# Two layers of spatial attention over 32 images: lane 1 normalised when its rows are split, and attended on two tiles at a time

## The chip, the cores and the metric

The kernel runs on one core of one Trainium2 chip. The metric is the device time of one execution in microseconds (us). Before the change three runs gave 1569.89, 1571.02 and 1573.38 us, with a median of 1571.02 us. The core has TensorE for matrix products (PE in the rows of a profile; its weight loads are PEld), VectorE (DVE), ScalarE (ACT), GpSimd (POOL) and SyncE (SP). Each engine takes its own instructions in order, and they meet at semaphores. Here SP does nothing but issue DMAs.

## The reference

The input is x of shape (32, 128, 32, 32): 32 images, 128 channels (C), 1024 positions (N). Two layers follow one another on each image:

```
h    = group_norm(x, 32 groups) * gn_w + gn_b
q,k,v = split(qkv_w @ h + qkv_b)                    # 128 channels each
attn = softmax(q^T k * 128**-0.5, over keys)        # 1024 x 1024
x1   = x + proj_w @ (v attn^T) + proj_b

q,k  = Wq @ x1 + bq, Wk @ x1 + bk                   # 16 channels each
v    = Wv @ x1 + bv                                 # 128 channels
attn = softmax(q^T k, over keys)                    # 1024 x 1024
out  = x1 + gamma * (v attn^T)
```

Operands of the large products are split into a half-precision head and a half-precision tail (value minus head), and a product takes three matmuls: head by head, head by tail, tail by head.

## The kernel before

**Tiles.** A tile is 128 queries of one image in one layer: 8 tiles for an image in a layer, 512 in all. For a tile the kernel makes 128 x 1024 scores in PSUM, their row maximum, the exponent, a head and a tail of the exponents in half precision (`rows`, 128 x 2048), a DMA transpose of those rows into `pt` with the keys in partitions, and the product of `pt` with the values into `mixed`.

**Lanes and slots.** The program is laid out by hand in slots. In a slot each of two lanes starts one tile. Lane 0 holds layer 0 and lane 1 holds layer 1 of an earlier image, except in the first eight slots (layer 0 of images 0 and 1 on both lanes) and the last eight (layer 1 of images 30 and 31 on both lanes). A tile of slot s has its scores made by PE at the end of slot s-1, its rows in slot s, its transpose issued by SP in slot s (lane 1) or s+1 (lane 0), and its product in slot s+3 (`ATTEND`). There it is also normalised and turned back, and in slot s+4 (`ADD`) it is added to the residual. One image of each layer takes eight slots.

**Lane 1 in a slot.** The scores stay in the PSUM tile `scores1` until the rows are done. `row_max` (DVE, line 572) takes the maximum, `exponent1` (ACT, line 457) writes the exponents over the scores, `head_row1` (ACT, line 465) writes the head with the constant factor 4096, `tail_row1` (DVE, line 589) writes the tail. Only then may PE write the next tile's scores: `score1` waits on `row_tailed[1]` through `scores_free` (line 785).

**Lane 0 in a slot.** `row_max` and `exp_bias` (DVE, lines 572 and 578), `exponent0` (ACT, line 452) into `prob`, and the head and the tail on POOL (lines 353 and 358).

**The product.** `attend` (PE, lines 823 to 825) has 8 blocks of keys by 3 matmuls. The transposed rows are the stationary operand and the values with a column of ones are the moving one, 129 or 128 columns wide. The queries come out in partitions, and the ones' column gives the row sum. `invert` (DVE, line 584) takes its reciprocal, `norm` (ACT, line 481) scales 128 x 128 values, `back` (PE, line 843) turns them so that channels are in partitions, and `x1_out` or `y_out` (DVE, lines 599 and 609) adds the residual.

**Order on the engines.** DVE in a slot: maximum of lane 1; tail of a projection of the slot before (`W`: lines 642, 649, 657); maximum and bias of lane 0; the adds of both lanes; `tail_row1`; the reciprocals; half of the statistics of a later image (`STATS`, line 616, in two of eight slots); small group-norm steps (`GN`, in two more). ACT: `exponent1`, `head_row1`, `exponent0`, then copies and `norm`s, then evictions of projections. PE: both products of slot-3, a projection of the values or of layer 1, a projection of q or k, group-norm products, the scores of the next slot, the turns back. Image 2 is an exception: its group-norm products stand behind the scores of slots 0 and 1 (`GN_BEHIND`).

**Buffers.** `pt` has 4 places in each lane (`RING`), `rows` has 3 in each.

## Time and profile before

| | |
|---|---|
| three runs, median | 1571.02 us |
| the profiled execution | 1575.76 us, its span 1573.7 us |
| mean granted TensorE clock | 0.989 |
| busy in the span | PE 94%, PEld 71%, DVE 82%, ACT 77%, POOL 79% |
| DMA queue of SP (transposes) | 1066688 packets, 270.42 MB |
| chain that ended last | SP's queue 66%, PE 17%, issue 5%, DVE 4% |

The profile is of one execution. Its page gives the busy share of each engine, the chain of work that ended last, followed back from the end, and the costliest groups of instructions by source line. The trace behind it can be asked for single instructions in order of time, for who waited for whom, and for the busy time of a stretch. Matmuls overlap in their records, so a matmul's duration is not the time it takes from the next one; the distance between two starts is.

### The profile page before, as it was taken

Reading aid. Unit: us, or ns where it says so; the run is one execution under the profiler, and the core shown is the slowest. Engines: PE = TensorE matmul, PEld = TensorE weight load, DVE = VectorE, ACT = ScalarE, POOL = GpSimd, SP = SyncE. Lnnn points to the kernel's source line nnn. Section 1 sums busy time; section 2 is a strip of 40 time slices with the busy share of each in tenths; the row PEclk is TensorE's granted clock in tenths of the full one; section 3 lists DMA queues with packets and bytes.
Section 4 is the critical chain, followed back from the end, with each engine's and each line's share of the span. In section 5 each row is a group of like instructions: output and inputs, shape, how many; then the busy total and the mean of one; then the engine's idle time right before and its main releaser. Section 6 shows DMA issues by size and latency. Waiting matters only on the chain.

```text
span 1573.7 us, 43918 instructions
## 1 busy us (share of the span) xinstructions
PE 1482.2 (94%) x16777; PEld 1116.9 (71%) x16777; DVE 1285.6 (82%) x2508; ACT 1218.2 (77%) x1698; POOL 1240.4 (79%) x1027
## 2 busy tenths in 40 slices
PE   4899999999999999999899999999999999999977
PEld 2577777776777777777677777677777777777766
DVE  5678888888888888888788888888888878888885
ACT  3578878887877887878788887887878878888774
POOL 3788888888878887878788888788788878888653
PEclk9899999999999999999999999999999999999999
DMA  3799999999999999999999999999999999999999
GB/s 76 135 161 199 203 197 204 198 206 204 198 195 194 207 203 203 202 193 209 189 202 211 202 194 202 196 202 203 195 199 210 203 190 204 203 193 199 192 200 181
DMA packets 1081437, 305.21 MB, mean 194 GB/s; under 512 B 1068272, under 2 KB 1068944, under 8 KB 1081232
## 3 DMA queue, kind: packets, MB, share of 16 engines
q1 hardware_dynamic: 1066688, 270.42, 105.4%
q10 hardware_dynamic: 14544, 31.99, 6.0%
q8 instruction: 137, 2.24, 0.5%
q14 instruction: 68, 0.56, 0.1%
HBM read 17.13 MB, written 16.78 MB: 22 GB/s over the span
## 4 chain that ended last, share of the span: by engine, by line
SPq 66%; PE 17%; issue 5%; DVE 4%; DMA 3%; ACT 2%; POOL 1%; DVEq 0%; POOLq 0%; ACTq 0%
SPq L299 66%; DMA pt<-rows 3%; PE mixed L823 3%; PE mixed L825 3%; PE mixed L824 3%; PE scores L778 2%; DVE nmax L572 2%; PE scores L779 1%; PE scores L780 1%; DVE rows L589 1%; PE scores L808 1%; PE bank_w L889 1%; PE bank_w L897 1%; ACT scores L457 1%; POOL rows L358 1%
## 5 line engine op out<-in xcount | busy, mean ns | idle before, releaser
L823 PE MATMUL mixed<-v_head,pt 128*128 128x129 f16 x4096 | 719.5, 222 | 35.7 <-DMA pt<-rows 34.6
L572 DVE TENSOR_REDUCE nmax<-scores 128x1 f32<-128x1024 f32 x512 | 620.5, 1217 | 154.8 <-PE scores L808 141.8
L825 PE MATMUL mixed<-v_head,pt 128*128 128x129 f16 x4096 | 718.7, 220 | 0.0
L824 PE MATMUL mixed<-v_tail,pt 128*128 128x128 f16 x4096 | 718.7, 219 | 0.0
L358 POOL TENSOR_TENSOR rows<-prob,rows 128x1024 f16<-128x1024 f32 x256 | 545.4, 2130 | 21.3
L353 POOL TENSOR_SCALAR rows<-prob 128x1024 f16<-128x1024 f32 x256 | 267.9, 1046 | 233.4 <-ACT prob L452 229.9
L457 ACT ACTIVATE scores<-scores,nmax 128x1024 f32<-128x1024 f32 x256 | 278.7, 1089 | 204.2 <-DVE nmax L572 204.2
L823 PEld LDWEIGHTS mixed<-v_head,pt 128*128 128x128 f16 x4096 | 399.0, 97 | 47.1 <-DMA pt<-rows 45.6
L824 PEld LDWEIGHTS mixed<-v_tail,pt 128*128 128x128 f16 x4096 | 405.7, 99 | 2.3
L825 PEld LDWEIGHTS mixed<-v_head,pt 128*128 128x128 f16 x4096 | 397.0, 97 | 0.0
L589 DVE SCALAR_TENSOR_TENSOR rows<-scores,rows 128x1024 f16<-128x1024 f32 x256 | 313.0, 1222 | 35.6 <-ACT rows L465 35.4
L452 ACT ACTIVATE prob<-scores,ebias 128x1024 f32<-128x1024 f32 x256 | 283.9, 1109 | 2.1 <-DVE ebias L578 2.1
L465 ACT ACTIVATE rows<-scores 128x1024 f16<-128x1024 f32 x256 | 262.2, 1024 | 24.8 <-ACT scores L457 1.5
L481 ACT ACTIVATE normal<-mixed,rinv 128x128 f32<-128x128 f32 x512 | 162.5, 364 | 101.6 <-DVE rinv L584 99.8
L778 PE MATMUL scores<-qk_head 128*128 128x512 f16 x512 | 198.6, 388 | 8.2 <-DVE rows L589 6.9
L779 PE MATMUL scores<-qk_tail,qk_head 128*128 128x512 f16 x512 | 196.2, 383 | 0.0
L780 PE MATMUL scores<-qk_head,qk_tail 128*128 128x512 f16 x512 | 196.0, 383 | 0.0
L420 POOL TENSOR_TENSOR qk_tail<-qk,qk_head 128x512 f16<-128x512 f32 x124 | 143.7, 1159 | 10.3
L778 PEld LDWEIGHTS scores<-qk_head 128*128 128x128 f16 x512 | 50.0, 98 | 97.9 <-issue 55.9
L808 PE MATMUL scores<-qk 64*128 64x512 f16 x512 | 98.9, 386 | 20.3 <-DVE rows L589 17.8
L843 PEld LDWEIGHTS bank_t<-ident,normal 128*128 128x128 f32 x512 | 71.6, 141 | 55.5 <-ACT normal L481 5.2
L843 PE MATMUL bank_t<-ident,normal 128*128 128x128 f32 x512 | 99.4, 275 | 3.8 <-ACT normal L481 3.7
(110 smaller groups left out, 1852.8 us busy)
## 6 DMA issues: line engine op xcount, KB each, us to landing
out_dram<-y ACTq DMA_DIRECT2D x64, 256.0 KB, 3.8
x_raw<-in_x_dram ACTq DMA_DIRECT2D x29, 512.0 KB, 5.2
pt<-rows SPq DMA_TRANSPOSE x512, 5.4
x_raw<-in_x_dram SPq DMA_DIRECT2D x3, 512.0 KB, 4.4
w_qkv<-in_L_conv_qkv_w_dram SPq DMA_DIRECT2D x3, 64.0 KB, 4.1
b_qk<-in_L_conv_bk_dram SPq DMA_DIRECT2D x8, 0.1 KB, 2.3
b_qk<-in_L_conv_bq_dram SPq DMA_DIRECT2D x8, 0.1 KB, 1.9
w_proj<-in_L_conv_proj_w_dram SPq DMA_DIRECT2D x1, 64.0 KB, 4.8
```

The costliest lines, as they stand in the source:

```text
L299: sp.dma_start_transpose(pt[l][:, i % RING, :, :], rows[l][:, i % ROWS, :, :].rearrange("p s n -> p (s n)")).then_inc(swung[l][i % RING], 16)
L353: nc.gpsimd.tensor_scalar(rows[0][:, tile.i % ROWS, 0, :], prob[:, tile.i % 2, :], 1.0, 1.0, ALU.mult, ALU.mult).then_inc(row_headed[0], 1)
L358: nc.gpsimd.tensor_tensor(rows[0][:, tile.i % ROWS, 1, :], prob[:, tile.i % 2, :], rows[0][:, tile.i % ROWS, 0, :], ALU.subtract).then_inc ...
L452: nc.scalar.activation(prob[:, tile.i % 2, :], scores[0][:, :], ACT.Exp, bias=ebias[:, tile.i % TILES:tile.i % TILES + 1], scale=1.0).then ...
L457: nc.scalar.activation(scores[1][:, :], scores[1][:, :], ACT.Exp, bias=nmax[1][:, tile.i % TILES:tile.i % TILES + 1], scale=1.0).then_inc( ...
L465: nc.scalar.activation(rows[1][:, tile.i % ROWS, 0, :], scores[1][:, :], ACT.Copy, scale=P_UP).then_inc(row_headed[1], 1)
L572: nc.vector.reduce_max(nmax[l][:, tile.i % TILES:tile.i % TILES + 1], scores[l][:, :], AX.X, negate=True).then_inc(maxed[l], 1)
L589: nc.vector.scalar_tensor_tensor(out=rows[1][:, tile.i % ROWS, 1, :], in0=scores[1][:, :], scalar=P_UP, in1=rows[1][:, tile.i % ROWS, 0, : ...
L778: mm(dst, a_head, b_head, start=start, stop=False)
L823: mm(mixed[l][:, 0:C + 1], head, vh[:, p, m, 0:C + 1], start=(m == 0), stop=False)
L824: mm(mixed[l][:, 0:C], head, vt[:, p, m, :], start=False, stop=False)
L825: done = mm(mixed[l][:, 0:C + 1], tail, vh[:, p, m, 0:C + 1], start=False, stop=(m == TILES - 1))
```

## The change

The exponent of lane 1 also gives its row sum. ACT scales the sum by 1/4096, DVE takes the reciprocal, and the head and the tail of a row are written with that reciprocal as their factor instead of the constant 4096, so the rows are already normalised (times 4096). The product of lane 1 takes two tiles at once. The values are the stationary operand, and the transposed rows of both tiles, 256 columns, are the moving one. Channels come out in partitions, and there is no reciprocal, no scaling and no turn back after it. Its first four key blocks are done in slot s+3 of the pair's second tile, the other four in slot s+4, and then one DVE instruction scales by 1/4096 and adds the residual for both tiles. The ring of lane 1 has 6 places. Lane 0 keeps its form. DVE's order in a slot changes: both maxima stand first, then the new reciprocal of lane 1, lane 0's add, the projection's tail, `tail_row1`, lane 0's reciprocal and the pair's add. Image 2's statistics and group-norm products move from slots -1, 0 and 1 to slots -3, -2 and -1, ahead of the scores, and its load is issued ahead of the sixteen small bias loads.

```diff
-RING = 4
+RING = (4, 6)
-STATS = Steps(-12, -11, first={1: (-11, -11), 2: (-9, -9)})
-GN = Steps(-10, -9, first={2: (-8, -7)})
+STATS = Steps(-12, -11, first={1: (-11, -11), 2: (-11, -11)})
+GN = Steps(-10, -9)
...
             def exponent1(tile):
+                at = slice(tile.i % TILES, tile.i % TILES + 1)
                 act.wait_ge(maxed[1], tile.i + 1)
-                nc.scalar.activation(scores[1][:, :], scores[1][:, :], ACT.Exp,
-                                     bias=nmax[1][:, tile.i % TILES:tile.i % TILES + 1],
-                                     scale=1.0).then_inc(exped[1], 1)
+                nc.scalar.activation(scores[1][:, :], scores[1][:, :], ACT.Exp, bias=nmax[1][:, at], scale=1.0,
+                                     accum_out=row_sum[:, at]).then_inc(exped[1], 1)
+                act.wait_ge(exped[1], tile.i + 1)
+                nc.scalar.activation(sum_down[:, at], row_sum[:, at], ACT.Copy,
+                                     scale=1.0 / P_UP).then_inc(summed_down, 1)
             def head_row1(tile):
...
-                act.wait_ge(exped[1], tile.i + 1)
+                act.wait_ge(inverted[1], tile.i + 1)
                 nc.scalar.activation(rows[1][:, tile.i % ROWS, 0, :], scores[1][:, :], ACT.Copy,
-                                     scale=P_UP).then_inc(row_headed[1], 1)
+                                     scale=rinv[1][:, tile.i % TILES:tile.i % TILES + 1]).then_inc(row_headed[1], 1)
...
+            def invert1(tile):
+                at = slice(tile.i % TILES, tile.i % TILES + 1)
+                dve.wait_ge(summed_down, tile.i + 1)
+                nc.vector.reciprocal(rinv[1][:, at], sum_down[:, at]).then_inc(inverted[1], 1)
             def tail_row1(tile):
...
-                nc.vector.scalar_tensor_tensor(out=rows[1][:, tile.i % ROWS, 1, :], in0=scores[1][:, :], scalar=P_UP,
+                nc.vector.scalar_tensor_tensor(out=rows[1][:, tile.i % ROWS, 1, :], in0=scores[1][:, :],
+                                               scalar=rinv[1][:, tile.i % TILES:tile.i % TILES + 1],
...
+            def add_pair(pair):
...
+                dve.wait_ge(attended[1], pair[1].i // 2 + 1)
+                nc.vector.scalar_tensor_tensor(out=of_pair(into, pair),
+                                               in0=mixed[1][:, 0:2 * C].rearrange("p (t c) -> p t c", c=C),
+                                               scalar=1.0 / P_UP, in1=of_pair(residual[:, tile.p, :], pair),
+                                               op0=ALU.mult, op1=ALU.add).then_inc(done, 2)
...
             def body(slot):
                 if tile := TILE_AT[1].get(slot):
                     row_max(tile)
+                if tile := TILE_AT[0].get(slot):
+                    row_max(tile)
+                    exp_bias(tile)
+                if tile := TILE_AT[1].get(slot):
+                    invert1(tile)
+                for tile in single_adds(slot):
+                    add_turned(tile)
                 for im, part in W.at(slot - 1):
...
-                if tile := TILE_AT[0].get(slot):
-                    row_max(tile)
-                    exp_bias(tile)
...
                 if tile := TILE_AT[1].get(slot):
                     tail_row1(tile)
-                for lane in TILE_AT:
-                    if tile := lane.get(slot - ATTEND):
-                        invert(tile)
+                if tile := TILE_AT[0].get(slot - ATTEND):
+                    invert0(tile)
+                for pair in pair_adds(slot):
+                    add_pair(pair)
                 for im, h in STATS.at(slot):
...
+            def attend_pair(pair, half):
...
+                into = mixed[1][:, 0:2 * C].rearrange("p (t n) -> p t n", n=C)
+                for m in range(half * PER_HALF, (half + 1) * PER_HALF):
+                    done = split_product(into, vh[:, p, m, 0:C], vt[:, p, m, :], pt[1][:, r:r + 2, m, :],
+                                         pt[1][:, r:r + 2, TILES + m, :], start=(m == 0), stop=(m == TILES - 1))
+                if half == 1:
+                    done.then_inc(attended[1], 1)
```

## Rows read from the trace of the kernel before

**Rows 1.** Waits of SP's queue: who waited, total us, times, longest.

```profile
SPq L295 <- DVE rows L589: 36.9, 6, 16.0
SPq L295 <- POOL rows L358: 16.3, 10, 3.0
```

**Rows 2.** All transposes at their line: count, ns min/median/max, first and last start.

```profile
L299 SPq DMA_TRANSPOSE pt<-rows x512: 1316/2720/7005, 29.0 to 1561.2; - x171
```

**Rows 3.** DVE in order of time, slots 9 and 249: start, us, instruction.

```profile
95.72 1.23 DVE L572 TENSOR_REDUCE nmax<-scores 128x1 f32<-128x1024 f32 x1 [1.48 <-PE scores L808]
...
1511.11 2.35 DVE L572 TENSOR_REDUCE nmax<-scores 128x1 f32<-128x1024 f32 x2 [0.55 <-PE scores L808]
```

**Rows 4.** DVE in order of time, one slot of 5.21 us.

```profile
106.75 1.23 DVE L572 TENSOR_REDUCE nmax<-scores 128x1 f32<-128x1024 f32 x1 [0.47 <-PE scores L808]
...
108.48 1.22 DVE L572 TENSOR_REDUCE nmax<-scores 128x1 f32<-128x1024 f32 x1
109.73 0.15 DVE L578 TENSOR_SCALAR ebias<-nmax 128x1 f32<-128x1 f32 x1
...
110.24 1.23 DVE L589 SCALAR_TENSOR_TENSOR rows<-scores,rows 128x1024 f16<-128x1024 f32 x1
...
111.96 1.23 DVE L572 TENSOR_REDUCE nmax<-scores 128x1 f32<-128x1024 f32 x1 [0.41 <-PE scores L808]
```

**Rows 5.** ACT in order of time, the same slot.

```profile
108.00 1.09 ACT L457 ACTIVATE scores<-scores,nmax 128x1024 f32<-128x1024 f32 x1 [0.64 <-DVE nmax L572]
109.19 1.02 ACT L465 ACTIVATE rows<-scores 128x1024 f16<-128x1024 f32 x1
```

**Rows 6.** ACT in order of time, the set-up: its smallest instruction.

```profile
5.92 0.20 ACT L558 ACTIVATE warm<-minus_half 128x1 f32<-128x1 f32 x1
```

**Rows 7.** Groups by line and shape: count, busy us, mean ns, idle before.

```profile
L490 ACT ACTIVATE qk<-bank_t,b_q 128x512 f32<-128x512 f32 x62 | 43.0, 694 | 0.3
...
L599 DVE TENSOR_TENSOR x<-bank_t,xb 128x128 f32<-128x128 f32 x256 | 73.9, 291 | 1.2 <-issue 0.6
...
L513 ACT ACTIVATE v_head<-bank_w 128x512 f16<-128x512 f32 x64 | 38.2, 597 | 0.5
```

**Rows 8.** DVE in order of time: slots with statistics and group-norm steps.

```profile
822.19 1.23 DVE L572 TENSOR_REDUCE nmax<-scores 128x1 f32<-128x1024 f32 x1 [1.38 <-PE scores L808]
...
828.46 1.23 DVE L572 TENSOR_REDUCE nmax<-scores 128x1 f32<-128x1024 f32 x1 [0.68 <-PE scores L808]
...
831.96 1.23 DVE L589 SCALAR_TENSOR_TENSOR rows<-scores,rows 128x1024 f16<-128x1024 f32 x1
...
833.24 0.67 DVE L616 BATCH_NORM_STATS2 stats<-x_raw 128x6 f32<-128x512 f32 x1
...
834.18 2.30 DVE L572 TENSOR_REDUCE nmax<-scores 128x1 f32<-128x1024 f32 x2
...
839.28 0.16 DVE L629 COPY gs<-bank_t 128x1 f32<-128x1 f32 x1 [0.29 <-PE bank_t L912]
...
839.73 1.21 DVE L572 TENSOR_REDUCE nmax<-scores 128x1 f32<-128x1024 f32 x1
```

**Rows 9.** PE in order of time, one slot: products, then turns back, then products.

```profile
800.38 0.22 PE L823 MATMUL mixed<-v_head,pt 128*128 128x129 f16 x1
...
803.11 0.22 PE L778 MATMUL bank_w<-w_head,h_head 128*128 128x128 f16 x1
...
806.15 0.38 PE L843 MATMUL bank_t<-ident,normal 128*128 128x128 f32 x2
...
806.37 0.22 PE L823 MATMUL mixed<-v_head,pt 128*128 128x129 f16 x1
```

**Rows 10.** DVE in order of time, the first slots.

```profile
34.65 0.16 DVE L629 COPY gs<-bank_t 128x1 f32<-128x1 f32 x1 [5.71 <-PE bank_t L912]
...
35.68 2.35 DVE L572 TENSOR_REDUCE nmax<-scores 128x1 f32<-128x1024 f32 x2
...
48.27 1.21 DVE L572 TENSOR_REDUCE nmax<-scores 128x1 f32<-128x1024 f32 x1
```

More of the change, by code:

```diff
@@ L40 @@
 SWING, ATTEND, ADD = (1, 0), 3, 4
+KEY_HALVES = (ATTEND, ATTEND + 1)
 FIRST_SLOT = -16
@@ L271, in swings, with of_pair @@
         def swings(tile):
-            return 16 * (tile.i // RING + 1)
+            return 16 * (tile.i // RING[tile.lane] + 1)
+        def of_pair(image, pair):
+            first, step = pair[0].t, pair[1].t - pair[0].t
+            tiles = image.rearrange("p (t c) -> p t c", c=C)
+            first %= tiles.shape[1]
+            return tiles[:, first:first + step + 1:step, :]
         def qk_bank(im, j):
@@ L530, in body @@
                     qk1_copy(im, h)
-                for lane in range(2):
-                    if tile := TILE_AT[lane].get(slot - ATTEND):
-                        norm(tile)
+                if tile := TILE_AT[0].get(slot - ATTEND):
+                    norm(tile)
                 for im, part in W.at(slot):
```

158 lines of the change are left out of this document (88 added, 70 removed).

## The prediction

> **What bounds the kernel now.** I read the chain of waits first. Two thirds of it lie in SP's queue, so the next view is that queue. From 29.0 to 1561.2 us it issues 512 transposes [rows 2], and in all that time it waits only 36.9 + 16.3 = 53.2 us for rows that are not ready, 16 times [rows 1]. The DMA path therefore paces the kernel: (1532.2 - 53.2) / 511 = 2.894 us a transpose, 5.79 us for the two of a slot. The measured slot is a little longer: lane 1's maxima of slots 9 and 249 start 1415.39 us apart [rows 3], 5.897 us over 240 slots. These 240 slots are 90% of the span, and the prediction turns on what becomes of the 5.897.
>
> The second question is how close the engines are to that pace, since a bound that lies 0.1 us under the next is no protection. One loop matters most. The scores of lane 1 lie in a single PSUM tile, which is written by PE, then read by the maximum, the exponent, the head and the tail, and only then may PE write it again. Rows 4 and 5 show this loop at its shortest, with nothing but itself to wait for. The maximum starts at 106.75, the exponent at 108.00 (1.25 later), the head at 109.19 (1.19), the tail at 110.24 (1.05, right behind the head), the next maximum at 111.96 (1.72, of which 1.23 are the tail and 0.49 PE's scores with their handoffs) [rows 4, 5]. The sum is 5.21 us. So today the loop has 0.69 us to spare against 5.897. PE is the other near bound: in the slot that starts at 822.19 its work is long enough that the next maximum starts 6.27 us later [rows 8]. The average of PE, however, lies below the pace, as a queue that never runs dry shows [rows 1].
>
> **Part 1, PE.** Today 48 matmuls of the two lanes take from 800.38 to 803.11, 2.73 us, 57 ns each [rows 9]. Lane 1's 24 a slot become 12 with 256 columns. If time goes by columns, nothing is won. If 128 columns at 2.4 GHz (53 ns) is the moving part and the rest of the 57 is fixed, 12 x 0.110 us replace 1.37 us and 0.05 us are won. The turn back of lane 1 goes: two of them took 0.22 us (806.15 to 806.37), so 0.11 [rows 9]. PE saves 0.11 to 0.16 us a slot, I take 0.16. It is off the path where the loop sets the pace. The weight loads that go are hidden today.
>
> The page "TensorE: Matmul & The Clock Gate" of the Trainium skill, section "Back-to-back issue gap", gives about 81 ns a matmul for streams of load and matmul with 128 columns, so that fewer and wider ones would save far more. The rows show 57 ns, so I go by them.
>
> **Part 2, the loop of lane 1.** Between exponent and head there now stand four things. (a) The read-out of the row sum. No row shows one. It costs 0 if it is part of the exponent, and at most one smallest instruction with its wait, 0.20 us [rows 6] and 0.10 us (the exponent ends at 109.09, the head starts at 109.19) [rows 5], so 0 to 0.29. I take 0.15, between the ends, as nothing is nearer to one of them. (b) The scaling of the sum: 128 x 1 on ACT, 0.20 [rows 6]. (c) The reciprocal on DVE, as the bias instruction of the same shape, 0.15 [rows 4]. (d) Two more handoffs between engines at 0.03 each, as from the head's end at 110.21 to the tail [rows 4, 5]. Besides, the head takes its factor from a pointer: on ACT an instruction with a pointer (694 ns) stands against one without (597 ns) at the same 512 elements [rows 7], so 0.10. For the tail on DVE no row has this pair. It lies between 0 and the same 0.10, and I take 0.05. In all 0.15 + 0.20 + 0.15 + 0.06 + 0.10 + 0.05 = 0.71, and the loop becomes 5.92 us. Its ends are 5.21 + 0.41 = 5.62 (read-out and pointers free) and 5.21 + 0.90 = 6.11.
>
> DVE could bind it as well. Two maxima (2 x 1.23), the bias with its handoff (0.18) and the reciprocal (0.15) free the head at 2.82, against 1.25 + 1.19 + 0.15 + 0.20 + 0.03 + 0.15 = 2.97 by ACT. ACT ends last, by 0.15. Lane 0's add (0.29 [rows 7]) and the projection's tail stand between the reciprocal and `tail_row1`. They take about as long as the head that DVE waits for, so they cost nothing. That is the cover they need.
>
> The page "VectorE: DVE Perf Modes" of the Trainium skill, section "Two Vector instructions with no wait between them", says that an accumulator output makes two instructions of one. If that held on ACT, (a) would be 0.20 rather than 0.15, and the sum below would be 12 us higher. No row here can show it.
>
> **Part 3, what stands behind the tail on DVE.** The 0.49 us from the tail's end to the next maximum hide up to 0.49 us of DVE work. The pair's add costs 0.42 (0.291 for 128 elements [rows 7], and 1.22 for 1024 [rows 4], so 1.04 ns an element). It stands behind one short reciprocal in every second slot and just fits. It no longer fits where statistics follow. In one slot of eight the statistics' second half held the maximum until 0.99 us after the tail's end at 833.19 [rows 8]; with one reciprocal less that is 0.92, 0.43 over the cover. The slot before it has pair add and first half (0.67 [rows 8]), some 1.14, 0.65 over. The next has the group-norm steps, 0.45 (839.28 to 839.73 [rows 8]), behind a pair add, 0.97, 0.48 over. These 1.56 us per image were mostly covered as long as the loop had room; now they add to it. In one further slot PE's work, 6.27 - 0.16 = 6.11 us, stays longer than the loop and adds 0.19.
>
> **Part 4, the sum.** An image takes 8 x 5.92 + 1.56 + 0.19 = 49.1 us, 6.14 us a slot. Against 5.897 that is +0.24, over 240 slots +58 us. The queue of SP is then no longer the bound, since its own pace is 5.79.
>
> The fill. Today DVE sits 5.71 us idle in front of a group-norm step of image 2 that PE makes behind the scores, and only at 35.68 does the maximum of slot 1 follow; the next is at 48.27, behind another such step and the last set-up work [rows 10]. With the steps ahead of the scores the first goes 2 us earlier, the second another 4. On the other side stand about 1.3 us for the statistics (2 x 0.67) ahead of slot 0, 0.7 us for the longer loop in some six slots, and the value projections of slots 2 and 3, which share one bank whose tail DVE now reads later. I take -3 us, between -7 and +2.
>
> The end. Eight slots with the longer loop give some +3 us, since they run under the pace today. The backlog of SP's queue is gone, -2.7 us by the lane-0 rows' lead, and the second key half stands between the last products and the last add. Together +1.
>
> The span becomes 1573.7 + 58 - 3 + 1 = 1629.7 us. Its own execution took 1575.76 us, 2.1 more than its span, and the median of the runs is 4.7 us below that. So I predict **1627 us**.
>
> **Rivals.** (1) The DMA stays the bound. If read-out and pointers are free and DVE's small work finds gaps, an image takes 8 x 5.62 + 1.56 + 0.49 (the slot of PE) = 47.0 us, 5.88 a slot, and nothing moves but the fill: 1571 - 3 = 1568 us. For it speaks a queue that never ran dry [rows 1]; against it, that three small instructions in a chain with handoffs have never cost nothing in this trace. 10%.
>
> (2) Faster. PE's waits, not the DMA, stretch the slot from 5.79 to 5.897, and with 0.16 us less work PE lets the queue run at its own pace: 0.107 x 240 = 26 us and the fill, 1542 us. It decides only if the loop with what stands behind it stays under 5.79 a slot, that is, if the additions come to less than about 0.36 us, while (b), (c) and (d) alone are 0.41. 7%. The figure that the TensorE page gives would speak for this one.
>
> (3) Slower still. The projection's tail moves from between the maxima to behind the reciprocal. It ends near 4.0 us after the maximum, about when PE has done its products (rows 9: they start 1.4 us after the maximum and last 2.7). Where two projections follow in neighbouring slots, four of eight, PE waits for it. Were it 0.3 us late, that is 0.15 us a slot, 36 us, 1663 us. 8%.
>
> **How the numbers follow.** The forecast has 75%. Its own range is 1590 (loop 5.75) to 1668 (loop 6.11, 50.4 us an image, +98 us). Rival 3 lies inside its upper half. To leave out no more than 2 in 10 the range must take in rival 1 below, so 1565 to 1668. Outside are rival 2 and some 6% above. A difference of 0.2%, 3 us, is about what a measurement of this kernel can tell from none. Rival 1 lies on that edge and counts half as faster and half as same: faster 12%, same 5%, slower 83%.
>
> **What would show it.** Lane 1's exponent to head should take 1.75 to 2.0 us instead of 1.19, and the maxima of lane 1 should start 5.9 to 6.0 us apart in plain slots and 6.3 to 6.6 in the three with statistics and group norm. SP's queue should wait for rows in most slots, hundreds of times instead of 16, and PE's product should hardly wait for DMA. Slot 1's maximum should start near 34 us and slot 2's near 42. I am wrong if exponent to head takes under 1.6 us, if lane 1's scores follow the tail at more than 0.5 us in plain slots (then PE or DMA binds), or if SP's waits stay few.

## The result and the profile after

The changed kernel takes **1637.78 us**, the median of four runs (1636.28 to 1641.17), beside 1570.64 us for the kernel before in the same job (1569.89 to 1573.38). The ratio is 1.0427, with a 95% interval of 1.0406 to 1.0449. The profiled execution took 1636.74 us, of which 1634.7 are its span: 61 us more than the 1573.7 of the kernel before.

Where the time went can be read from the starts of lane 1's maxima. Up to slot 9 the new kernel is 0.5 us later (96.24 against 95.72, rows 3), the 240 slots from 9 to 249 take 58.4 us more (1473.83 against 1415.39), and all behind slot 249 takes 2.0 us more. So the question is the steady slot: 6.141 us instead of 5.897.

Waits of SP's queue in the changed kernel (who waited, for whom, total us, times, longest) answer to [rows 1]:

```profile
SPq L331 <- DVE rows L630: 151.9, 130, 20.3
SPq L331 <- POOL rows L394: 122.2, 116, 3.8
```

The queue that waited 16 times now waits 246 times for rows, 274 us in all. It no longer sets the pace, and PE no longer waits for its transposes (PE's waits for `pt`, before and after):

```profile
PE mixed L823 <- DMA pt<-rows: 34.6, 34, 4.5
...
PE mixed L877 <- DMA pt<-rows: 2.8, 1, 2.8
```

What sets the pace is seen in the waits of the engines:

```profile
DVE rows L630 <- ACT rows L504: 150.7, 256, 1.2
PEld scores L862 <- DVE rows L630: 128.0, 173, 1.6
PE scores L862 <- DVE rows L630: 118.5, 128, 2.6
...
ACT rows L504 <- DVE rinv L626: 75.1, 256, 0.6
...
DVE rinv L626 <- ACT sum_down L497: 16.2, 85, 1.5
PE scores L862 <- ACT qk L539: 14.3, 30, 1.4
```

PE waits for the tail, the tail for the head, the head for the reciprocal: the loop of lane 1's scores, closed. The chain in one slot, ACT in order of time (start, us, instruction, idle before), answers to [rows 5]:

```profile
847.39 1.09 ACT L494 ACTIVATE scores<-scores,nmax 128x1024 f32<-128x1024 f32 x1 [1.35 <-DVE nmax L609]
848.40 0.19 ACT L494 ACTIVATION_READ_ACCUMULATOR scores<-scores,nmax 128x1 f32 x1
848.63 0.20 ACT L497 ACTIVATE sum_down<-row_sum 128x1 f32<-128x1 f32 x1
849.12 1.11 ACT L504 ACTIVATE rows<-scores,rinv 128x1024 f16<-128x1024 f32 x1 [0.29 <-DVE rinv L626]
```

DVE in the same slot answers to [rows 4]:

```profile
846.13 1.22 DVE L609 TENSOR_REDUCE nmax<-scores 128x1 f32<-128x1024 f32 x1 [0.18 <-PE scores L862]
847.53 1.22 DVE L609 TENSOR_REDUCE nmax<-scores 128x1 f32<-128x1024 f32 x1 [0.18 <-PE scores L834]
...
848.86 0.16 DVE L626 RECIPROCAL rinv<-sum_down 128x1 f32<-128x1 f32 x1
...
850.27 1.28 DVE L630 SCALAR_TENSOR_TENSOR rows<-scores,rinv,rows 128x1024 f16<-128x1024 f32 x1 [1.05 <-ACT rows L504]
...
852.15 1.23 DVE L609 TENSOR_REDUCE nmax<-scores 128x1 f32<-128x1024 f32 x1 [0.53 <-PE scores L862]
```

Maximum to exponent 1.26, exponent to head 1.73 (1.19 before), head to tail 1.15 (1.05), tail to next maximum 1.88 here and 1.77 at its shortest (1.72). The shortest of the 240 slots takes 5.90 us; the prediction had 5.92 for the loop.

The 240 slots fall into eight classes, by the slot's place in an image (slot number modulo 8). This table gives the median time from one maximum of lane 1 to the next, worked out from the starts of L572 before and L609 after:

```
place        0     1     2     3     4     5     6     7    sum
before     5.99  5.41  5.59  6.24  6.27  5.72  5.55  5.48  46.2
after      6.33  5.95  6.19  6.02  6.33  6.34  6.12  5.90  49.2
over 5.90  0.43  0.05  0.29  0.12  0.43  0.44  0.22  0.00   2.0
```

The sums are those of the medians. After, the mean of all slots is 49.1, as good as the same. Before, it is 47.2, because 28 of the 240 slots took over 0.3 us more than their median, 30 us in all; those are about as many as PE's waits for a transpose. Before, slots of 5.4 us also made up for slots of 6.2. After, no slot is under 5.9.

### The profile page after: what moved, and what is told of

Same layout as the page of the kernel before. It is cut to its first block, busy times and chain, and to the rows that moved or that the text cites. A ratio compares the mean times of both kernels' runs of the same rounds, so it can differ in the third digit from the quotient of the medians.

```text
span 1634.7 us, 37051 instructions
## 1 busy us (share of the span) xinstructions
PE 1437.1 (88%) x13449; PEld 1026.2 (63%) x13449; DVE 1313.6 (80%) x2380; ACT 1252.5 (77%) x1954; POOL 1238.8 (76%) x1027
## 4 chain that ended last, share of the span: by engine, by line
PE 35%; DVE 30%; ACT 26%; issue 8%; DMA 1%; ACTq 0%; POOLq 0%; DVEq 0%; POOL 0%; SPq 0%
DVE nmax L609 12%; ACT rows L504 11%; DVE rows L630 11%; ACT scores L494 7%; PE scores L832 6%; PE scores L834 5%; PE scores L833 4%; PE scores L862 4%; ACT prob L488 2%; ACT h_head L546 2%; PE mixed L877 2%; PE mixed L879 2%; PE mixed L878 2%; PE bank_w L967 2%; PE mixed L832 2%
## 5 line engine op out<-in xcount | busy, mean ns | idle before, releaser
L609 DVE TENSOR_REDUCE nmax<-scores 128x1 f32<-128x1024 f32 x512 | 617.4, 1219 | 106.6 <-PE scores L862 67.3
L630 DVE SCALAR_TENSOR_TENSOR rows<-scores,rinv,rows 128x1024 f16<-128x1024 f32 x256 | 328.6, 1283 | 150.7 <-ACT rows L504 150.7
L877 PE MATMUL mixed<-v_head,pt 128*128 128x129 f16 x2048 | 365.0, 222 | 5.2 <-DMA pt<-rows 2.8
L879 PE MATMUL mixed<-v_head,pt 128*128 128x129 f16 x2048 | 364.9, 220 | 0.0
L878 PE MATMUL mixed<-v_tail,pt 128*128 128x128 f16 x2048 | 364.8, 218 | 0.0
L504 ACT ACTIVATE rows<-scores,rinv 128x1024 f16<-128x1024 f32 x256 | 285.3, 1115 | 75.1 <-DVE rinv L626 75.1
L832 PE MATMUL mixed<-pt,v_head 128*128 128x256 f16 x1024 | 279.6, 273 | 0.0
L833 PE MATMUL mixed<-pt,v_head 128*128 128x256 f16 x1024 | 279.6, 273 | 0.0
L834 PE MATMUL mixed<-pt,v_tail 128*128 128x256 f16 x1024 | 279.4, 273 | 0.0
L862 PE MATMUL scores<-qk 64*128 64x512 f16 x512 | 99.3, 386 | 154.0 <-DVE rows L630 118.5
L877 PEld LDWEIGHTS mixed<-v_head,pt 128*128 128x128 f16 x2048 | 199.6, 97 | 20.7 <-issue 3.6
L878 PEld LDWEIGHTS mixed<-v_tail,pt 128*128 128x128 f16 x2048 | 202.3, 99 | 2.3
L879 PEld LDWEIGHTS mixed<-v_head,pt 128*128 128x128 f16 x2048 | 197.9, 97 | 0.0
L862 PEld LDWEIGHTS scores<-qk 64*128 64x128 f16 x512 | 27.2, 93 | 229.2 <-DVE rows L630 128.0
L519 ACT ACTIVATE normal<-mixed,rinv 128x128 f32<-128x128 f32 x256 | 94.1, 368 | 92.2 <-DVE rinv L620 90.6
```

What stands on the lines that cost most here:

```text
L504: nc.scalar.activation(rows[1][:, tile.i % ROWS, 0, :], scores[1][:, :], ACT.Copy, scale=rinv[1][:, tile.i % TILES:tile.i % TILES + 1]).th ...
L609: nc.vector.reduce_max(nmax[l][:, tile.i % TILES:tile.i % TILES + 1], scores[l][:, :], AX.X, negate=True).then_inc(maxed[l], 1)
L630: nc.vector.scalar_tensor_tensor(out=rows[1][:, tile.i % ROWS, 1, :], in0=scores[1][:, :], scalar=rinv[1][:, tile.i % TILES:tile.i % TILES ...
L832: mm(dst, a_head, b_head, start=start, stop=False)
L833: mm(dst, a_head, b_tail, start=False, stop=False)
L834: return mm(dst, a_tail, b_head, start=False, stop=stop)
```

## Experiments

"To head" is the time from the start of lane 1's exponent to the start of its head.

**The chain, alone and taken out.** The first kernel is the changed one without the chain, so that it leaves out the division of lane 1's rows (its edit stands below). The second is the kernel before with nothing but the chain.

```diff
-                nc.scalar.activation(scores[1][:, :], scores[1][:, :], ACT.Exp, bias=nmax[1][:, at], scale=1.0,
-                                     accum_out=row_sum[:, at]).then_inc(exped[1], 1)
-                act.wait_ge(exped[1], tile.i + 1)
-                nc.scalar.activation(sum_down[:, at], row_sum[:, at], ACT.Copy,
-                                     scale=1.0 / P_UP).then_inc(summed_down, 1)
+                nc.scalar.activation(scores[1][:, :], scores[1][:, :], ACT.Exp, bias=nmax[1][:, at],
+                                     scale=1.0).then_inc(exped[1], 1)
...
-                                     scale=rinv[1][:, tile.i % TILES:tile.i % TILES + 1]).then_inc(row_headed[1], 1)
+                                     scale=P_UP).then_inc(row_headed[1], 1)
...
-                                               scalar=rinv[1][:, tile.i % TILES:tile.i % TILES + 1],
+                                               scalar=P_UP,
...
-                if tile := TILE_AT[1].get(slot):
-                    invert1(tile)
```

> The changed kernel with the chain between exponent and head taken out: no row sum, no scaling, no reciprocal of lane 1; head and tail have the constant factor 4096 again, so lane 1's rows are not normalised (that division is left out). Products in pairs, DVE's order and the fill stay as in the change. Theory (the loop of lane 1's scores sets the pace): exponent to head returns to 1.18 us, the plain loop to 5.2 to 5.6, the queue of SP is full again and paces the kernel at 5.79 to 5.90 a slot: 1550 to 1575 us. Rival (the wide products or DVE's new order cost the time): it stays above 1620 us.

> The kernel before with the chain alone: row sum, scaling, reciprocal, and head and tail with that factor; the reciprocal stands behind lane 0's bias on DVE. Products, turns back, DVE's old order and the fill are those of before. Theory: exponent to head takes 1.73 us or more, and since the projection's tail still stands between the two maxima, the reciprocal comes 0.3 us later still in six of eight slots; 6.4 us a slot, 1665 to 1715 us, slower than the change itself. Rival (the products in pairs are the cause): under 1600 us. Rival (the chain is hidden if DVE keeps its old order): about 1571 us.

Measured: without the chain 1558.04 us, ratio 0.991 [0.9884, 0.9936]; with nothing but the chain 1695.97 us, ratio 1.0793 [1.0778, 1.0809]. The first goes to head in 1.18 us again, its slot takes 5.796 us, and SP's queue hardly waits:

```profile
SPq L331 <- DVE rows L627: 32.7, 10, 19.5
SPq L331 <- POOL rows L394: 23.7, 16, 3.8
```

So the chain costs the changed kernel 80 us, more than the whole change does: everything else in it (wider products, no turn back, DVE's order, the longer ring, the fill) is worth 13 us against the kernel before.

It looks as if 5.796 us were the pace of 5.79 that the prediction worked out for the queue alone. The waits of SP's queue between 96 and 1500 us say otherwise (the kernel before, then this one):

```profile
SPq L295 <- POOL rows L358: 5.3, 2, 3.0
...
SPq L331 <- POOL rows L394: 4.9, 4, 2.3
SPq L331 <- DVE rows L627: 0.4, 1, 0.4
```

In its steady slots the queue was hardly ever short of rows in either kernel, so its own pace there is that of the slots, 5.90 us before and 5.80 here. The 5.79 came out because the prediction's division also takes in the start, where 16 transposes went out by slot 9. The same division gives 5.66 us for this kernel, 2 x (1534.1 - 32.5 - 56.4) / 511. Both kernels are paced by the DMA queue, and each has its own pace.

What the rest of the change did can be seen apart from that. The typical slot (the mean of the eight medians) falls from 5.78 to 5.63 us, by about what PE saves. The slots in which PE waits for a transpose add 0.12 us to the mean before and 0.17 here (PE waits 34 times before, 46 times here). Both figures are of single executions: the profiled one of this kernel is the fastest of four (1549.36 us), that of the kernel before is 4 us above its median, and the medians lie only 13 us apart. Why the queue was quicker is open, and PE's smaller load was not tried by itself.

The second kernel shows what DVE's old order would cost. DVE in one of its slots, where the projection's tail still stands between the two maxima:

```profile
944.30 1.21 DVE L579 TENSOR_REDUCE nmax<-scores 128x1 f32<-128x1024 f32 x1
945.42 0.68 DVE L670 TENSOR_TENSOR v_tail<-bank_w,v_head 128x512 f16<-128x512 f32 x1
946.02 1.22 DVE L579 TENSOR_REDUCE nmax<-scores 128x1 f32<-128x1024 f32 x1
...
947.34 0.15 DVE L597 RECIPROCAL row_inv<-sum_down 128x1 f32<-128x1 f32 x1
...
948.74 1.28 DVE L601 SCALAR_TENSOR_TENSOR rows<-scores,row_inv,rows 128x1024 f16<-128x1024 f32 x1 [0.86 <-ACT rows L472]
```

The reciprocal stands behind 0.6 us of projection, and exponent to head is 2.0 to 2.1 us in such slots, five of eight. The steady slot is 6.370 us. Order and wider products together take 0.23 us of that off; they were not parted.

**The fill alone**: the kernel before with image 2's statistics and group-norm steps in the new slots, its load earlier, and the steps ahead of the scores.

> The kernel before with the fill alone: image 2's statistics and group-norm products in slots -3, -2 and -1, its load ahead of the small bias loads. Theory: slot 9 starts 2 to 5 us earlier and the steady slots stay at 5.90 us, so 1566 to 1569 us, as far as SP's queue does not take the gain back. Rival (the fill gains nothing, as what leaves one wait comes back in the next): 1571 us.

Measured: 1568.54 us, ratio 0.9982 [0.996, 1.0003]. The maxima of slots 0, 1, 2 and 9 start at 27.81, 34.04, 42.16 and 90.22 (before 24.29, 35.68, 48.27, 95.72). The moves do save 5.5 us by slot 9, but the median falls by 3 us only, and the interval includes 1. The DMA queue paces this kernel too (2.3 us of waits between 96 and 1500 us). That it takes the gain back is my reading; one execution doesn't show it, for the times of this kernel spread from 1562 to 1578 us.

**One more small instruction**, a second scaling of the row sum into a spare tile, inside the chain (the edit below) or behind the head.

```diff
                 act.wait_ge(exped[1], tile.i + 1)
+                nc.scalar.activation(sum_spare[:, at], row_sum[:, at], ACT.Copy, scale=1.0 / P_UP)
                 nc.scalar.activation(sum_down[:, at], row_sum[:, at], ACT.Copy,
                                      scale=1.0 / P_UP).then_inc(summed_down, 1)
```

> The changed kernel with the scaling of the row sum done twice on ACT, the first time into a spare tile, between exponent and head. Theory (it lies in the loop): each of 256 slots grows by one such instruction, 0.20 us at the most where ACT's side of the chain decides: +40 to +55 us, 1678 to 1693 us. Rival (ACT's chain is covered by DVE's maximum of lane 0, or the DMA paces): 1638 us.

> The changed kernel with one more scaling of lane 1's row sum by ScalarE in each slot, into a spare tile nobody reads, issued right behind the head of lane 1's rows instead of inside the chain. The same work was added inside the chain before, and cost 25 us (0.10 us a slot). Chain theory: in five or six of eight slots ScalarE stands idle behind the head until lane 0's exponent may start, so 0.1 to 0.2 us there costs nothing; only the slots in which ScalarE's work behind the head (lane 0's exponent and the copy of queries and keys) is itself awaited, slot 0 and slot 2 of an image, give up to 0.1 us each: 30 x 0.2 = 6 us, 1640 to 1650 us. Rival, ScalarE's whole load sets the time: wherever the instruction stands it costs the same 25 us, 1660 us or more.

Measured: inside 1663.11 us, ratio 1.0582 [1.0567, 1.0597]; behind 1641.97 us, ratio 1.0445 [1.0415, 1.0474]. The same instruction costs 25 us in one place and at most 4 in the other; the load of ACT is the same in both. Those 4 us are hardly clear of the spread of single runs: the intervals overlap, and the 240 slots take 2 us more. Behind the head only slot 0 is longer (6.33 to 6.42), where ACT's next work is itself awaited. Inside, I had expected twice as much. ACT inside the chain shows why:

```profile
915.37 0.19 ACT L495 ACTIVATION_READ_ACCUMULATOR scores<-scores,nmax 128x1 f32 x1
915.60 0.20 ACT L498 ACTIVATE sum_spare<-row_sum 128x1 f32<-128x1 f32 x1
915.71 0.19 ACT L499 ACTIVATE sum_down<-row_sum 128x1 f32<-128x1 f32 x1
916.18 1.11 ACT L506 ACTIVATE rows<-scores,rinv 128x1024 f16<-128x1024 f32 x1 [0.29 <-DVE rinv L628]
```

Two instructions of 0.20 us that don't depend on each other start 0.11 us apart. Exponent to head grew by 0.09 us. So what a small instruction adds to this chain is its spacing where it follows another, and more only where somebody waits for its result.

**The scaling left out**: the reciprocal is taken of the row sum itself, and the pair's sum is multiplied by 1.

> The changed kernel with lane 1's rows left at the size of the plain exponent over its sum, so that ScalarE's scaling of the sum (0.20 us) is not needed, VectorE's reciprocal waits for the exponent itself, and the sum of the pair is multiplied by 1 instead of 1/4096; the low half of a row then keeps less of its precision, the function is the same. Theory that both branches tie: the scaling ended at 848.83 us in one slot and VectorE, busy with lane 0's maximum, was free at 848.86, so taking the scaling away gives 0.03 us there; it gives more, 0.16 to 0.19 us, only in the 85 slots of 256 where the reciprocal was seen to wait for the scaling: 85 x 0.17 + 171 x 0.03 = 20 us at the most, some of it already covered by the order of VectorE: 1617 to 1630 us. Rival, the prediction's step (b), a link of 0.20 us in all slots: 256 x 0.20 = 51 us, 1587 us.

Measured: 1610.82 us, ratio 1.0248 [1.0222, 1.0274]. That is 27 us less, between my two theories. It is a matter of slots. In the places 2, 5, 6 and 7 the head comes 0.20 to 0.23 us earlier (1.53 and 1.50 us), in 0, 1, 3 and 4 not at all (1.72). DVE in one slot of each kind, first place 3, then place 6:

```profile
881.17 1.22 DVE L604 TENSOR_REDUCE nmax<-scores 128x1 f32<-128x1024 f32 x1 [0.18 <-PE scores L857]
882.57 1.22 DVE L604 TENSOR_REDUCE nmax<-scores 128x1 f32<-128x1024 f32 x1 [0.18 <-PE scores L829]
...
883.90 0.15 DVE L621 RECIPROCAL rinv<-row_sum 128x1 f32<-128x1 f32 x1
...
899.61 2.30 DVE L604 TENSOR_REDUCE nmax<-scores 128x1 f32<-128x1024 f32 x2
901.94 0.15 DVE L610 TENSOR_SCALAR ebias<-nmax 128x1 f32<-128x1 f32 x1
902.05 0.16 DVE L621 RECIPROCAL rinv<-row_sum 128x1 f32<-128x1 f32 x1
```

In the first, lane 0's scores are 0.18 us late behind lane 1's maximum. The second maximum ends then, and the reciprocal starts 2.73 us after the first maximum, whatever ACT does. In the second both maxima follow without a gap, the reciprocal starts 2.44 us after the first, and ACT's scaling had been the later of the two. (In place 2 the exponent itself starts 0.2 us late, so that ACT's branch is the later one in spite of the gap.) The two branches change places from slot to slot, so the scaling counts in half the slots.

**The copy of queries and keys ahead of lane 0's exponent** on ACT, twice an image, in the places 0 and 4.

> The changed kernel with ScalarE's copy of an image's queries and keys put ahead of lane 0's exponent instead of behind it, once an image. Theory: the first score product of the next image waited for this copy, which stood behind the exponent of lane 0 and that behind the head, now later: this is the 0.42 us that slot 0 of an image lost beyond the prediction. With the copy ahead slot 0's period falls from 6.33 to about 5.9 us: 31 x 0.42 = 13 us, 1625 us. Rival: lane 0's exponent, then 0.5 us later, delays its head and VectorE's tail of lane 0, so that the next maximum of lane 1 is late by the same: no gain, 1635 to 1645 us, and the 0.42 us is found in slot 7 or 1 instead.

Measured: 1632.67 us, ratio 1.0386 [1.0362, 1.041]. Place 0 falls from 6.33 to 5.91 as expected, but place 1 takes back 0.14: lane 0's scores are later there (its maximum starts 1.55 us after lane 1's, in place of 1.40). Place 4 keeps its 6.33. Over the 240 slots that is 9 us; slot 9 comes 2.5 us later and the end takes 1.4 us more in the profiled execution, so 5 us are left of the expected 13. The mechanism was right, a part of it only moved.

**The statistics ahead of the tail**, in DVE's idle stretch of 1.05 us, in places 3 and 6; and the three edits together.

```diff
-STATS = Steps(-12, -11, first={1: (-11, -11), 2: (-11, -11)})
+STATS = Steps(-13, -10, first={0: (-12, -11), 1: (-11, -11), 2: (-11, -11), 3: (-12, -11)})
...
+                stats_now = STATS.at(slot)
+                if not W.at(slot - 1):
+                    for im, h in stats_now:
+                        gn_first(im, h)
+                    stats_now = []
                 if tile := TILE_AT[1].get(slot):
                     tail_row1(tile)
...
-                for im, h in STATS.at(slot):
+                for im, h in stats_now:
```

> The changed kernel with the two statistics instructions of an image (0.68 us each, and the aggregate behind the second) taken out of slots 4 and 5, where they stand between the tail of lane 1's rows and the next maximum, and put ahead of the tail in the slots 3 and 6 that have no projection's tail; there VectorE was seen idle for 1.05 us, waiting for the head. Chain theory: slot 4 falls from 6.33 to about 6.0 us (the pair's sum of 0.40 us stays behind the tail, under the 0.49 us of the next score's way), slot 5 from 6.34 to 5.9, slots 3 and 6 keep theirs: 30 x 0.76 = 23 us, 1615 us. Rival: VectorE's sum of work sets the pace, or the statistics run into the next step wherever they stand: 1630 us or more.

> The changed kernel with three edits together: no scaling of the row sum (alone 27 us), the copy of queries and keys ahead of lane 0's exponent (alone 5 us), and the statistics in the idle stretch ahead of the tail (expected 23 us alone). They touch different slots or different links, so they should add up: 1638 - 27 - 5 - 23 = 1583 us, and the exponent-to-tail loop at some 5.93 us a slot is still over the DMA queue's own pace of 5.80. Rival: one of them only moved a wait onto another, and the sum is 10 us or more short of that, 1593 us or more. Lane 1's rows are not scaled by 4096 here.

Measured: 1626.45 us, ratio 1.0332 [1.0311, 1.0354], and for the three together 1601.46 us, ratio 1.0176 [1.0155, 1.0196]. Alone the edit takes 0.24 us from place 4 and 0.43 from place 5 and adds 0.05 in place 6. Over the 240 slots that is 15 us (steady slot 6.078). Slot 9 comes 2.3 us later and the end takes 3.5 us more, so 9 us are left in the span and 11 between the medians, of the expected 23. The later start need not be the edit's doing: slot 1 comes at 37.0 us here and at 36.4 with the one small instruction behind the head, but at 34.7 in the changed kernel. One execution of each can't part this from chance. Together the three give 36 us, neither the expected 55 nor the 43 that they gave one by one. So the rival holds here. In the kernel with all three, exponent to head is 1.72 us again in the places 5 and 6, where the scaling's absence had made it 1.50. With the statistics gone from behind the tail, lane 0's scores are late for DVE there too (its two maxima stand 1.40 us apart in place of 1.14), and DVE's branch is the longer one. One edit had undone what the other needed.

**Another way to divide.** Here rows are made as before, and the factor reaches the product by a detour off the chain: ACT multiplies a tile of ones by the reciprocals, PE turns it, and DVE takes the product times the turned factors, plus the residual.

```diff
+                nc.scalar.activation(spread[:, tile.i % 4, :], ones[:, :], ACT.Copy,
+                                     scale=rinv[1][:, tile.i % TILES:tile.i % TILES + 1]).then_inc(spread_out, 1)
...
+                nc.vector.tensor_copy(product[:, :], mixed[1][:, 2 * C:4 * C]).then_inc(multiplied, 1)
+                dve.wait_ge(multiplied, pair[1].i // 2 * 2 + 1)
+                nc.vector.scalar_tensor_tensor(out=product[:, :], in0=mixed[1][:, 0:2 * C], scalar=1.0 / P_UP,
+                                               in1=product[:, :], op0=ALU.mult, op1=ALU.mult).then_inc(multiplied, 1)
+                dve.wait_ge(multiplied, pair[1].i // 2 * 2 + 2)
+                nc.vector.tensor_tensor(of_pair(into, pair), product[:, :].rearrange("p (t c) -> p t c", c=C),
+                                        of_pair(residual[:, tile.p, :], pair), ALU.add).then_inc(done, 2)
...
+                        nc.tensor.transpose(mixed[1][:, (2 + j) * C:(3 + j) * C], spread[:, tile.i % 4, :],
+                                            ident[:, :]).then_inc(spread_turned, 1)
```

> The changed kernel with the factor of lane 1's rows taken off the chain, the wide value products kept: the head and the tail are made of 4096 times the exponent, as in the kernel before; VectorE's reciprocal of the row sum is no longer awaited by the head; two slots later ScalarE multiplies a tile of ones (128 x 128) by it, TensorE turns this tile, VectorE copies the turned pair of tiles out of PSUM, multiplies the product by it and adds the residual: three instructions over 128 x 256 in place of one for a pair, one ScalarE copy and one turn per tile. Chain theory: exponent to head falls from 1.73 to 1.18 us (1.30 if the read-out of the sum stands ahead of the head), the loop from 6.14 towards 5.2 to 5.4, so that it falls behind the DMA queue's own pace of 5.80: 1560 us if the added VectorE work (2 x 0.4 per pair, 0.4 us a slot) and ScalarE work (0.3 us a slot) find idle time, 1590 us if half of VectorE's stands ahead of a maximum. Rival, VectorE's and ScalarE's sum of work sets the pace: VectorE 80% + 0.4/6.1 = 87%, no gain from a shorter chain, 1640 us or more.

Measured: 1609.49 us, ratio 1.024 [1.0211, 1.0269]. The loop did what was expected: 1.30 us to head, so the read-out of the sum costs 0.12, and plain slots take 5.31 to 5.36 us. But the slots with the pair's three instructions take 6.2 to 6.9, for DVE has them all between tail and maximum, and 1609 us is more than the 1560 to 1590 that I expected:

```profile
853.15 0.40 DVE L671 COPY product<-mixed 128x256 f32<-128x256 f32 x1
853.59 0.42 DVE L673 SCALAR_TENSOR_TENSOR product<-mixed,product 128x256 f32<-128x256 f32 x1
854.12 0.42 DVE L676 TENSOR_TENSOR y<-product,x1b 128x256 f32<-128x256 f32 x1
```

Two kernels try to take work from there. In the first, ACT copies the factors; in the second they are turned a slot earlier, into lane 0's bank, and DVE copies them in the odd slots. Both also have the two moves tried above, the copy of queries and keys ahead of lane 0's exponent and the statistics ahead of the tail.

> The kernel with the factor turned on TensorE, and with VectorE relieved: ScalarE copies the turned pair of factors out of PSUM (about 0.5 us per pair) in place of VectorE, the statistics stand ahead of the tail, and the copy of queries and keys ahead of lane 0's exponent. In that kernel the plain slots took 5.31 to 5.36 us and the slots with the pair's three VectorE instructions 6.2 to 6.9 us. Chain theory: with 0.44 us less of VectorE's work behind the tail in every second slot, and the statistics gone from there, these fall to 5.7 to 6.2 us, the mean to 5.6 us, so that the DMA queue's own pace of 5.80 us sets the time: 98 + 240 x 5.80 + 70 = 1560 us, with waits of SyncE's queue few, faster than the kernel before. Rival: ScalarE, with 0.4 + 0.25 us more work a slot (88% of 5.8 us), now holds back lane 0's exponent and the norms, so that the tiles of lane 0 come late: 1585 us or more.

> The kernel with the factor turned on TensorE, with VectorE's three instructions of a pair spread over two slots: the factors are turned a slot earlier, ahead of lane 0's value product and in its bank, and VectorE copies them out behind the tail in the odd slots, where the first such kernel had nothing behind the tail and a period of 5.31 to 5.36 us; the even slots keep the product and the sum (0.53 + 0.34 us). The statistics stand ahead of the tail and the copy of queries and keys ahead of lane 0's exponent. No copy by ScalarE. Chain theory: the next score's way hides 0.49 us of VectorE's work behind the tail, so the odd slots keep 5.3 to 5.4 us (copy and reciprocal 0.42) and the even ones come to 5.33 + 0.87 - 0.49 = 5.7 us, 6.2 in the slot with the head of the normalised image, 6.5 in the one with the group's three small instructions; the mean is 45.6/8 = 5.70 us, below the DMA queue's own pace of 5.80, which then sets it: about 97 + 240 x 5.80 + 70 = 1560 us, faster than the kernel before (1571). Rival: lane 0's normalised rows and ScalarE's work behind them are 0.35 us later in every odd slot, and TensorE waits for the copy before lane 0's next value product, so that scores come late and the mean stays over 5.9 us: 1590 us or more.

Measured: with ACT's copy 1624.68 us, ratio 1.0317 [1.0296, 1.0339], slower than the kernel without these edits (1609.49). DVE's queue, here in place 4, shows it: the product waits for a copy that stands behind lane 0's exponent, and behind the product waits the next maximum.

```profile
850.83 0.16 DVE L639 RECIPROCAL rinv<-mixed 128x1 f32<-128x1 f32 x1
851.77 0.42 DVE L681 SCALAR_TENSOR_TENSOR product<-mixed,factor 128x256 f32<-128x256 f32 x1 [0.78 <-ACT factor L528]
```

It does so only where the copy of queries and keys (0.63 us) has been put ahead of that exponent: the slots are 7.06 us in the places 0 and 4 (6.16 and 6.89 without these edits), and in the places 2 and 6, where DVE finds its factors ready, they are 6.59 and 6.55 (6.61 and 6.52). So the loss belongs to the two edits together. ACT's copy alone was not tried.

With the earlier turn 1581.09 us, ratio 1.0072 [1.0058, 1.0086]: 57 us better than the changed kernel, and still slower than the kernel before. Its slot takes 5.902 us. I had reckoned with 5.70 by DVE's work alone; in place 3 I expected 5.3 to 5.4 us and found 5.97. There PE's own work ends last, as its order of time shows (the places 1 and 4 are also longer than expected, by 0.25 and 0.5 us, and were not followed up):

```profile
869.99 0.27 PE L861 MATMUL mixed<-pt,v_tail 128*128 128x256 f16 x1
870.09 1.02 PE L994 MATMUL bank_w<-x,w_qk_t 128*128 128x512 f32 x2
870.96 0.38 PE L859 MATMUL bank_t<-h_head,w_head 128*128 128x512 f16 x1
...
871.70 0.39 PE L889 MATMUL scores<-qk 64*128 64x512 f16 x2
```

The tail that frees the scores had ended at 870.98 (L640, 869.76 + 1.22), 0.72 us before PE came to them. With a short loop such a slot with two projections is bound by PE again, as it was before the change (6.24 us). Of all kernels here only the one without the division is measurably faster than the kernel before.

## Why the prediction was right, and where its terms were off

**The bound.** That the loop of lane 1's scores, with 0.69 us to spare, would replace the DMA queue is shown: SP's waits went from 16 to 246, PE's waits for a transpose from 34 to 1, the loop's shortest slot is 5.90, and without the chain the queue sets the pace again, at 5.796. One reading of the prediction was wrong here: 5.79 us was not the queue's own pace in the steady slots. That was 5.90, as the first experiment shows. The forecast did not rest on it, since the loop was compared with 5.897.

**The additions.** Exponent to head was predicted at 1.75 and is 1.73. Its links, from start to start in the rows above, are exponent to read-out 1.01, read-out to scaling 0.23, scaling to reciprocal 0.23, reciprocal to head 0.26. (a), the read-out, taken at 0.15, is 0.12 (1.30 against 1.18 where it alone was added). (b), (c) and (d) together, 0.41, are 0.43. The pointers cost 0.10 for the head and 0.06 for the tail (means 1115 against 1024 ns, 1283 against 1222), predicted 0.10 and 0.05. The sum is 0.71 predicted, 0.69 measured. One statement was wrong: that ACT's branch is the later one by 0.15. It took the two maxima end to end, but in five of eight places lane 0's scores come 0.18 us behind lane 1's maximum (its own starts at 1.40 in place of 1.22). It also took ACT's way to the reciprocal at 1.57 us, where 1.47 were measured, and the last link to the head at 0.18, where 0.26 were. So the branches tie, and without the scaling DVE's is the later in half the slots.

For (a) the prediction also weighed a rule of the Trainium skill ("VectorE: DVE Perf Modes", "Two Vector instructions with no wait between them"), that an accumulator output makes two instructions of one. The page says this of VectorE, and no run here has such an output there. On ACT the trace looks the same: the read-out has a row of its own with 0.19 us. It costs the chain less, 0.12, for it starts before the exponent's row ends (848.40 against 847.39 + 1.09 = 848.48).

**PE.** The products with 256 columns start 0.11 us apart, so 12 take 1.31 us in place of 1.37, and the turn back saves its 0.11: 0.17 us a slot, as predicted. The 81 ns a matmul that the Trainium skill gives ("TensorE: Matmul & The Clock Gate", "Back-to-back issue gap") would have made it far more; the rows don't show them.

**Work behind the tail.** Here single terms failed, and that their sum did not is luck. Predicted over the loop: 0.65, 0.43 and 0.48 us in the places 4, 5 and 6, and 0.19 for PE, 1.75 us an image. Measured over 5.90: 0.43, 0.44 and 0.22 there, 0.12 in place 3 and 0.05 in place 1. DVE behind the tail of a slot in place 4:

```profile
856.29 1.28 DVE L630 SCALAR_TENSOR_TENSOR rows<-scores,rinv,rows 128x1024 f16<-128x1024 f32 x1 [0.35 <-ACT rows L504]
857.49 0.16 DVE L620 RECIPROCAL rinv<-mixed 128x1 f32<-128x1 f32 x1
857.57 0.40 DVE L662 SCALAR_TENSOR_TENSOR y<-mixed,x1b 128x256 f32<-128x256 f32 x1
857.89 0.68 DVE L670 BATCH_NORM_STATS2 stats<-x_raw 128x6 f32<-128x512 f32 x1
858.49 2.37 DVE L609 TENSOR_REDUCE nmax<-scores 128x1 f32<-128x1024 f32 x2
```

From the tail's end (857.57) to the maximum are 0.92 us, where I had 1.14. I had added up durations, but each instruction starts before the row of the last one has ended: the reciprocal of 0.16 is followed after 0.08, the pair's sum of 0.40 after 0.32, the statistics of 0.68 after 0.60. Less the 0.49 of cover, 0.43 are left instead of 0.65. Missing in the prediction were 0.43 us in place 0 and 0.29 in place 2, ACT's side of the same question. I had asked what stands behind the delayed tail on DVE and not what stands behind the delayed head on ACT: in place 0 the copy that the next image's first scores wait for (PE L862 <- ACT qk L539, 30 times), in place 2 the head of the normalised image (1.24 us) ahead of the next exponent. That the copy is the cause in place 0 is shown by its experiment. For place 2 it is read from the trace, where maximum to exponent is 1.45 instead of 1.26; no run tried it. It was 1.55 before, so this wait was there already and hidden. The three terms behind the tail were 0.47 us too large together and the loop 0.02 us a slot; 0.72 us in the places 0 and 2 and 0.05 in place 1 were missing. These errors nearly cancel: an image takes 49.2 us by the medians, predicted 49.1.

**Fill and end.** Here the sum was off, by 3.5 and 1 us. Slot 1 came at 34.73 and slot 2 at 43.49 (forecast near 34 and 42), but slot 0 came 3.4 us later where I had 1.3, and slot 3 followed slot 2 by 8.75 us (before 7.13). The moves alone win 5.5 us by slot 9; the rest of the change takes 6.0 back (90.22 against 96.24), where the sum that gives -3 has 0.7 us for the longer loop once, not in each of six slots. Up to 2 us of this may be chance, as said at the statistics above. So of the 11 us between 1627 and 1638, 5 are in the span (1629.7 against 1634.7). The other 6 come from setting the median 4.7 us under the profiled run, as before; this kernel's median lies 1.0 us above it.

**The rivals.** The first (DMA stays the bound) and the second are refuted for the change as it is. The second has something in it once the chain is gone: 13 us are gained, and the typical slot is shorter by 0.15 us. But its premise, a queue with a pace of its own 0.1 us under the slot, is not borne out, for the queue was as seldom short of rows before as there. The third, PE waiting for the projection's tail, did not come: PE's waits for those tails come to 4.2 + 2.1 + 1.0 us in the whole execution.

**The signs.** Exponent to head and the queue's waits came as foretold, plain slots took 5.90 to 6.02 us, and PE's product waited for a transpose once. The scores followed the tail's end at 0.49 us in place 7, but at 0.53 and 0.60 in the places 1 and 3: in the slot of place 3 shown above the tail ended at 851.55 and PE came to the scores at 851.72, straight from its own products, so that there the loop does not bind alone. What delays place 1 is open: PE's waits there (30 times, 0.7 us) are for nothing that the profile shows. Of the three slots with statistics and group norm two took 6.33 and 6.34, the third 6.12, and place 0, which was not named, took 6.33.

## What to carry to other kernels

Where one buffer passes through several engines and back, add up that loop from start to start and compare it with the pace of the present bound: an instruction inside costs its spacing or its handoff in every round in which its branch is the later one (25 us here), and the same instruction beside it costs almost nothing (at most 4 us here). Then ask on every engine of the loop, not only on one, what stands in the queue behind the delayed instruction and who waits for that. Small gains inside such a loop need not add up where two branches tie (36 us here, not 43).

## What the runs showed of the hardware

Small instructions overlap on their engine: independent ones of 0.20 us on ACT start 0.11 us apart, of 0.15 us on DVE 0.07 to 0.11 apart. A row sum taken along with the exponent is a separate instruction of 194 ns that starts 1.01 us after the exponent of 1.09 us and holds up the next one by 0.12 us. Columns are what a product costs: at a granted clock of 0.995 half-precision matmuls with a weight load each start 0.109 us apart with 256 columns and 0.057 us with 128.

The pace of the transposes is not one number: over stretches of 32 slots the kernel before took 5.77 to 5.99 us a slot while its queue was hardly ever short of rows. Kernels paced by the queue also spread more from run to run (17 runs from 1568 to 1583 us before, 4 from 1549 to 1562 without the chain) than those paced by the loop (4 from 1694 to 1697 with the chain alone, 6 from 1609 to 1612 without the scaling).
